# Staggering the two sequences in the pooling passes of a macaron block on eight NeuronCores

## The chip, the cores and the metric

The kernel runs on all 8 cores of one Trainium2 chip. The batch of 16 sequences is split by sequence: each core gets two, runs the same program on them and exchanges nothing with the others. The metric is the device time in microseconds (us) of the slowest core.

## The reference

The input is x of [16, 4096, 1024] float32. Three layers follow one another: half a feed-forward block, attention, half a feed-forward block, each on a layer norm and each added to x.

```python
x = x + 0.5 * ffn(layernorm(x))
x = x + attn(layernorm(x))
x = x + 0.5 * ffn(layernorm(x))

# ffn: D 1024 -> M 64, each of the 64 widened to 16, relu, summed, -> 1024
# attn, per sequence, h = 16 heads of 64:
mixed_q = y @ Wq + bq;  mixed_k = y @ Wk + bk
q_w = softmax((mixed_q @ Wqa + bqa) * scale, axis=1)       # over 4096 tokens
pooled_q = einsum('bsh,bshd->bhd', q_w, mixed_q)           # one row of 1024
mixed_qk = mixed_k * pooled_q
k_w = softmax((mixed_qk @ Wka + bka) * scale, axis=1)
pooled_k = einsum('bsh,bshd->bhd', k_w, mixed_qk)
out = (pooled_k * mixed_q) @ Wt + bt + mixed_q
```

What matters here: the two softmaxes run over all tokens of a sequence, so pooled_q of a sequence is known only after a pass over all of its tokens, the key scores need pooled_q, the key softmax needs the maximum of all key scores, and the output needs pooled_k. The two sequences of a core don't depend on each other.

## The kernel before

Data lie transposed, with the 1024 features as 8 chunks of 128 partitions and the tokens along the free dimension, in tiles of T = 512. A sequence has 8 tiles. "par" is the sequence's number, 0 or 1, and picks its buffers.

The program is written as a list of operations. Each names the keys that it reads and writes; a small planner (Prog) turns them into semaphore waits: a reader waits for the last writer of its key, a writer waits for the last writer and all readers since. Nothing is reordered: each engine and each DMA-issuing queue executes its operations in the order in which the code adds them. So the order of the calls is the order on every engine.

The parts of the program:

1. A dense first part (p1_...): feed-forward, statistics, query scores, and the projections ptq and ptk, which are spilled to DRAM (ptq_d, ptk_d, 1 MB a tile); the query scores go to escq_d.
2. Query pooling (pbq_load, pbq_chain), for each tile: load ptq's tile (1 MB, line 846) and the reciprocal deviation r16 (16 KB, GpSimd's queue, line 482); load the scores esc (32 KB, line 857); ScalarE takes the exponential (line 583); VectorE makes eb (line 595); TensorE spreads eb over the partitions in 8 matmuls (line 601), each followed by a VectorE multiply with a sum (line 606); one add closes the chain (line 615).
3. p1_fin: turns the sums into pooled_q and scales Wka by it (into wkaq_s for sequence 0, wqa_s for 1); p2_init clears the sums.
4. Key scores (p2_load, p2a_chain), for each tile: load ptk's tile (line 931), 8 score matmuls (line 942), and on VectorE the scores, their maximum and the running maximum (lines 552, 556, 559).
5. eb2_final: the bias from the maximum. Key pooling (p2_load, p2b_chain): load ptk's tile again, the 8 score matmuls again, VectorE's esc (line 963), then the same exponential, eb and 8 multiplies as in the query pooling.
6. p2_fin: pooled_k and the output's bias, with 64 small matmuls (line 1010).
7. A dense last part (p3_...): output projection and second feed-forward, one sequence after the other.

In parts 2, 4 and 5 each pass of the loop over ti handles both sequences: it issues the load of tile ti and then runs the chain of tile ti-1, first for sequence 0, then for 1. Sequence 0's loads are issued by SyncE (SP), sequence 1's by ScalarE. The esc load of the query pooling stands in the chain, so on its queue it comes behind the 1 MB load of the next tile. The chain of tile ti-1 comes after the r16 load of tile ti in the order, and waits for it.

Each sequence alternates between two buffers: even tiles in a primary buffer (ptq_s or ptk_s), odd tiles in its half of big_s (tile_buf). The odd buffers of both sequences also share the key "wqT": a load into one half waits for the last load into and the readers of the other half, and a reader waits for both loads.

Of the kernel before, what the change touches and what calls it, by code (L numbers as in the profile page):

```python
# [16 lines left out]
NCH = 8  # L17
# [144 lines left out]
def build_nc(cfg: CFG, dbg=False, paranoid=False, only_p1=False):  # L162
# [60 lines left out]
    with ExitStack() as stk:  # L223
# [33 lines left out]
        ptq_s = sbt("ptq_s", [128, NCH, T], BF16)  # L257
# [311 lines left out]
        def eb2_final(si, side, bias2_ap, bias2_k, tag):  # L569
            base = (si * 2 + side) * 8  # L570
            rmf = base + (cfg.ntile % 2)
            V_op(lambda e: e.tensor_sub(tiny_s[:, base + 7:base + 8], bias2_ap,
                                        tiny_s[:, rmf:rmf + 1]),
                 ["rm%d_%d" % (base, cfg.ntile % 2), bias2_k],
                 ["mx%d" % base], tag + "_eb2")
# [265 lines left out]
        def pbq_load(si, ti):  # L841
            par = si % 2
            t0 = si * cfg.seq + ti * T
            ring = "sync" if par == 0 else "scalar"
            buf, bkeys = pbq_buf(par, ti)
            dma(ring, lambda e: e.dma_start(out=buf[:, :, :],
                                            in_=ptq_r[:, :, t0:t0 + T]),
                ["ptqd_%d" % t0] + bkeys, bkeys, "pbq_pld")
            bcast_r(1, t0, "r16_%d" % par, r16_s[:, par, :], H, "pbq_r16")

        def pbq_chain(si, ti):
            par = si % 2
            t0 = si * cfg.seq + ti * T
            buf, bkeys = pbq_buf(par, ti)
            ring = "sync" if par == 0 else "scalar"
            es = 2 * par + ti % 2
            dma(ring, lambda e: e.dma_start(out=esc_s[:, es, :],
                                            in_=escq_d[:, t0:t0 + T]),
                ["escd_%d" % t0, "escA%d" % es], ["escA%d" % es],
                "pbq_escld")  # L860
            pool_core(si, ti, par, 0, q_slot(si), t0,
                      "pbq_%d_%d" % (si, ti), buf, bkeys)
# [55 lines left out]
                 ["pb_sc", "bka2a"], ["bka2"], "p1_bka2")  # L918

        def p2_buf(par, ti):  # L920
            primary = ((ptk_s, ["ptk_%d" % j for j in range(NCH)])
                       if par == 0
                       else (ptq_s, ["ptq_%d" % j for j in range(NCH)]))
            return tile_buf(primary, par, ti)

        def p2_load(si, ti, tag):
# [259 lines left out]
        if not only_p1:  # L1186
            ti = cfg.ntile - 1
            for si in seqs:
                p1_D1(si, ti)
                p1_D2(si, ti)  # L1190
                for c in range(NCH):
                    p1_D3_j(si, ti, c)
                p1_D3sp(si, ti)
            for si in seqs:
                eb2_final(si, 0, bqa2_s[:], "bqa2", "p1eb2_%d" % si)
            for ti in range(cfg.ntile + 1):
                for si in seqs:
                    if ti < cfg.ntile:
                        pbq_load(si, ti)
                    if ti > 0:  # L1200
                        pbq_chain(si, ti - 1)
            for si in seqs:
                p1_fin(si)
            for si in seqs:
                p2_init(si)
            for ti in range(cfg.ntile + 1):
                for si in seqs:
                    if ti < cfg.ntile:
                        p2_load(si, ti, "p2a_%d_%d" % (si, ti))
                    if ti > 0:  # L1210
                        p2a_chain(si, ti - 1)
            for si in seqs:
                eb2_final(si, 1, bka2_s[:, si:si + 1], "bka2",
                          "p2eb2_%d" % si)
            for ti in range(cfg.ntile + 1):
                for si in seqs:
                    if ti < cfg.ntile:
                        p2_load(si, ti, "p2b_%d_%d" % (si, ti))
                    if ti > 0:
                        p2b_chain(si, ti - 1)  # L1220
            for si in seqs:
                p2_fin(si)
            for sidx, si in enumerate(seqs):
                p3_wtscale(si, reload=(sidx > 0))
                p3_load(si, 0)
                for ti in range(cfg.ntile):
                    if ti + 1 < cfg.ntile:
                        p3_load(si, ti + 1)
                    if ti == 0:
                        p3_wtblock(si, 0)  # L1230
                    else:
                        p3_B(si, ti - 1, filler=mk_p3_filler(si, ti))
                    p3_stats(si, ti)
                p3_B(si, cfg.ntile - 1)
        else:
            def cpout(e):
                return e.dma_start(out=out_d.rearrange("(c p) t -> p c t", p=128)[:, :, 0:T],
                                   in_=x1_bf[:, (cfg.ntile - 1) % 2, :, :])
            dma("gpsimd", cpout,
                ["x1bf%d_%d" % ((cfg.ntile - 1) % 2, j) for j in range(NCH)],  # L1240
                ["outst"], "p1only_out")
# [110 lines left out]
```

How the kernel before makes its waits and increments, by code:

```python
        def run_stream(eng_name, e, clear_sems=None, go=None):  # L118
            if eng_name == "gpsimd":
                for s in clear_sems or ():
                    e.sem_clear(s)
                if go is not None:
                    e.sem_inc(go, 1)
            elif go is not None:
                e.wait_ge(go, 1)
            waited = {}
            def wait_to(skey, val):
                if waited.get(skey, -1) < val:
                    e.wait_ge(sems[skey], val)
                    waited[skey] = val
# [9 lines left out]
                        wait_to((dep.eng, False), dep.val)  # L141
                if op.is_dma:
                    for (ln, occ) in op.lanes:
                        if occ > 1:
                            wait_to((eng_name, "d", ln), 16 * (occ - 1))
                ret = op.emit(e)
                insts = ret if isinstance(ret, (list, tuple)) else [ret]
                if op.is_dma:
                    assert len(insts) == op.ndma, (op.tag, len(insts), op.ndma)
                    for it, (ln, occ) in zip(insts, op.lanes):
                        it.then_inc(sems[(eng_name, "d", ln)], 16)
                elif op.need_inc:
                    insts[-1].then_inc(sems[(eng_name, False)], 1)
            for (eng2, ln), occ in lane_occ.items():
```

## Time and profile before

| | |
|---|---|
| time, 3 runs | 2500.36 us median (2489.80 to 2501.22) |
| profiled execution | 2521.51 us, span of its slowest core 2519.9 us (core 0) |
| spans of the cores | 2475.2 to 2519.9 us |
| TensorE busy (share of span) | 1784.0 us (71%) |
| VectorE busy | 1008.6 us (40%) |
| ScalarE busy | 528.7 us (21%) |
| DMA | 220.28 MB, mean 87 GB/s |
| mean granted TensorE clock, core 0 | 0.803 of full |

How to read it. The profile is one execution; the span is the time from a core's first to its last instruction. Busy shares are means over the whole span and hide that the parts differ. These two lines of the page show the span in 40 equal slices of 63 us, each digit the busy tenths of a slice:

```
PE   0558888888898888888934436666877875877785
DVE  0123333333333333333356524555443443444443
```

Parts 2 to 6 lie in the 20th to the 28th slice. PE is TensorE's matmuls, DVE VectorE, ACT ScalarE, POOL GpSimd, SP SyncE; SPq and ACTq are the DMA queues that SP and ACT issue to. L601 is line 601.

### The profile page before, as it was taken

Reading aid. Unit: us, or ns where it says so; the run is one execution under the profiler, and the core shown is the slowest. Engines: PE = TensorE matmul, PEld = TensorE weight load, DVE = VectorE, ACT = ScalarE, POOL = GpSimd, SP = SyncE. Lnnn points to the kernel's source line nnn. Section 1 sums busy time; section 2 is a strip of 40 time slices with the busy share of each in tenths; the row PEclk is TensorE's granted clock in tenths of the full one; section 3 lists DMA queues with packets and bytes.
Section 4 is the critical chain, followed back from the end, with each engine's and each line's share of the span. In section 5 each row is a group of like instructions: output and inputs, shape, how many; then the busy total and the mean of one; then the engine's idle time right before and its main releaser. Section 6 shows DMA issues by size and latency. Waiting matters only on the chain.

```text
span 2519.9 us, 22407 instructions; the slowest of 8 cores (2475.2 to 2519.9 us)
## 1 busy us (share of the span) xinstructions
PE 1784.0 (71%) x6340; PEld 584.5 (23%) x6340; DVE 1008.6 (40%) x1892; ACT 528.7 (21%) x662; POOL 37.1 (1%) x78
## 2 busy tenths in 40 slices
PE   0558888888898888888934436666877875877785
PEld 0212222222232222222300111112222221222221
DVE  0123333333333333333356524555443443444443
ACT  0232222221222222221000000001322321233232
POOL 0000000000000000000000000000000000000000
PEclk9868998888999999899955565556888876798786
DMA  9212222222112222211243462422224224142411
GB/s 151 61 50 68 84 85 68 84 84 84 45 66 77 85 85 85 68 52 51 64 143 106 140 192 80 115 72 93 71 72 140 73 56 149 52 132 71 130 46 67
DMA packets 174773, 220.28 MB, mean 87 GB/s; under 512 B 6176, under 2 KB 138528, under 8 KB 174016
## 3 DMA queue, kind: packets, MB, share of 16 engines
q1 hardware_dynamic: 126784, 160.15, 20.2%
q10 hardware_dynamic: 44448, 46.70, 5.8%
q0 software_dynamic: 3424, 12.00, 2.9%
q8 instruction: 58, 0.95, 0.2%
q14 instruction: 59, 0.48, 0.1%
HBM read 146.38 MB, written 84.44 MB: 92 GB/s over the span
## 4 chain that ended last, share of the span: by engine, by line
PE 62%; DVE 17%; issue 6%; DMA 6%; ACT 6%; DVEq 1%; ACTq 1%; SPq 0%; POOLq 0%; POOL 0%
PE pb L1063 10%; PE pb L773 9%; PE pb L805 9%; DVE h_bf L606 6%; PE pb L522 4%; PE pb L510 4%; PE pb L942 3%; DVE x_s L1154 3%; PE pb L491 3%; DVE x_bf L691 2%; ACT big_s L717 2%; DMA big_s<-ptk_d 2%; PE pb L725 2%; PE pb L1129 2%; PE pb L535 2%
## 5 line engine op out<-in xcount | busy, mean ns | idle before, releaser
L517 ACT ACTIVATE h_bf<-pb,b1f_s,w1f_s 128x512 bf16<-128x512 f32 x256 | 198.8, 777 | 466.0 <-PE pb L510 466.0
L601 PE MATMUL pb<-eb_s,esel_s 16*128 16x512 bf16 x256 | 141.7, 578 | 170.9 <-DVE eb_s L595 115.5
L773 PE MATMUL pb<-x_bf,wq_s 128*128 128x512 bf16 x1024 | 243.2, 380 | 0.0
L805 PE MATMUL pb<-x_bf,wk_s 128*128 128x512 bf16 x1024 | 243.2, 380 | 0.0
L535 PE MATMUL pb<-g_bf,wout_s 64*128 64x512 bf16 x256 | 129.5, 528 | 97.1 <-DVE x_s L1154 32.8
L816 DVE CAST ptk_s<-pb 128x512 bf16<-128x512 f32 x128 | 88.5, 691 | 270.7 <-PE pb L810 270.7
L522 PE MATMUL pb<-h_bf,w2bd_s 128*64 128x512 bf16 x256 | 110.0, 430 | 84.8 <-ACT h_bf L517 84.8
L1081 DVE TENSOR_TENSOR x_s<-pb,rf_s 128x512 f32<-128x512 f32 x128 | 88.5, 691 | 190.1 <-PE pb L1068 186.6
L1063 PE MATMUL pb<-ptq_s,wt_s 128*128 128x512 bf16 x512 | 132.8, 406 | 17.6 <-DMA ptq_s<-ptq_d 14.0
L784 DVE CAST ptq_s<-pb 128x512 bf16<-128x512 f32 x128 | 87.2, 690 | 137.9 <-PE pb L778 135.7
L1154 DVE SCALAR_TENSOR_TENSOR x_s<-pb,bout_s,x_bf 128x512 f32<-128x512 f32 x128 | 96.0, 750 | 106.2 <-PE pb L535 94.5
L510 PE MATMUL pb<-st_bf,sel_s 64*128 64x512 bf16 x256 | 106.3, 415 | 34.2 <-DVE st_bf L500 34.2
L434 DVE COPY stat_s<-pb 1x512 f32<-1x512 f32 x48 | 32.6, 679 | 241.8 <-PE pb L729 162.5
L1063 PE MATMUL pb<-ptk_s,wt_s 128*128 128x512 bf16 x512 | 129.3, 398 | 0.0
L583 ACT ACTIVATE ee_s<-esc_s,tiny_s 16x512 bf16<-16x512 f32 x32 | 23.0, 720 | 497.5 <-DVE esc_s L963 294.6
L805 PEld LDWEIGHTS pb<-x_bf,wk_s 128*128 128x128 bf16 x1024 | 89.7, 98 | 119.8 <-issue 29.1
L773 PEld LDWEIGHTS pb<-x_bf,wq_s 128*128 128x128 bf16 x1024 | 89.7, 98 | 119.7 <-issue 29.0
L691 DVE SCALAR_TENSOR_TENSOR x_bf<-pb,bout_s,x_s 128x512 bf16<-128x512 f32 x128 | 91.3, 748 | 59.9 <-PE pb L535 56.3
L725 PE MATMUL pb<-x_bf,ones_s 128*1 128x512 bf16 x128 | 54.3, 601 | 84.2 <-ACT big_s L717 84.2
L1092 ACT ACTIVATE big_s<-x_bf 128x512 bf16<-128x512 bf16 x128 | 80.6, 629 | 157.7 <-DVE x_bf L1086 157.5
L448 ACT ACTIVATE stat_s<-stat_s,eps_s 1x512 f32<-1x512 f32 x48 | 34.5, 719 | 344.7 <-DVE stat_s L443 344.6
L1086 DVE SCALAR_TENSOR_TENSOR x_bf<-x_s,btt_s,x_bf 128x512 bf16<-128x512 f32 x128 | 96.2, 751 | 16.3 <-DVE x_s L1081 3.5
(146 smaller groups left out, 1707.5 us busy)
## 6 DMA issues: line engine op xcount, KB each, us to landing
x_s<-xT SPq DMA_DIRECT2D x16, 2048.0 KB, 12.1
out<-x_s SPq DMA_DIRECT2D x16, 2048.0 KB, 8.2
x_d<-x_bf ACTq DMA_DIRECT2D x16, 1024.0 KB
ptq_d<-ptq_s SPq DMA_DIRECT2D x16, 1024.0 KB, 4.4
ptk_d<-ptk_s SPq DMA_DIRECT2D x16, 1024.0 KB, 4.6
x_bf<-x_d SPq DMA_DIRECT2D x16, 1024.0 KB, 14.2
ptq_s<-ptq_d SPq DMA_DIRECT2D x12, 1024.0 KB, 9.4
ptq_s<-ptk_d ACTq DMA_DIRECT2D x8, 1024.0 KB
```

Of the source, the lines that this page charges most:

```text
L510: T_op(lambda e, c=c, eb=eb: e.matmul(pb[eb][:], sel_s[:, c, :], st_bf[:, reg, :], start=True, stop=True), ["st%d" % reg, "sel"], ["pb_e%d ...
L517: S_op(lambda e, c=c, eb=eb: e.activation(out=h_bf[:, c % 2, :], in_=pb[eb][:], func=AF.Relu, bias=b1f_s[:, c:c + 1], scale=w1f_s[:, c:c + ...
L522: T_op(lambda e, c=c: e.matmul(pb[PB_FF][0:FM, :], w2bd_s[:, c, :], h_bf[:, c % 2, :], start=(c == 0), stop=(c == NCH - 1)), ["h%d" % (c % ...
L535: T_op(lambda e, j=j, wb=wb: e.matmul(pb[wb][:], wout_s[:, j * 128:(j + 1) * 128], g_bf[:], start=True, stop=True), ["g", "wout"], ["pb_w% ...
L601: T_op(lambda e, c=c, ebk=ebk: e.matmul(pb[ebk][:], esel_s[:, c, :], eb_s[:, par, :], start=True, stop=True), ["ebbf%d" % par, "esel"], [" ...
L606: V_op(lambda e, c=c, ebk=ebk: e.scalar_tensor_tensor(out=h_bf[:, 0, :], in0=buf[:, c, :], scalar=1.0, in1=pb[ebk][:], op0=ALU.mult, op1=A ...
L691: V_op(lambda e, j=j, wb=wb: e.scalar_tensor_tensor(out=x1_bf[:, par, j, :], in0=pb[wb][:], scalar=bout2_s[:, j:j + 1], in1=x_s[:, par, j, :],
L725: ins.append(e.matmul(pb[PB_S1][0:1, :], ones_s[:, 1:2], x1_bf[:, par, c, :], start=(c == 0), stop=(c == NCH - 1)))
L773: ins = [e.matmul(pb[wb][:], wq_s[:, kc, j * 128:(j + 1) * 128], x1_bf[:, par, kc, :], start=(kc == 0), stop=False) for kc in range(NCH)]
L805: ins = [e.matmul(pb[wb][:], wk_s[:, kc, j * 128:(j + 1) * 128], x1_bf[:, par, kc, :], start=(kc == 0), stop=False) for kc in range(NCH)]
L1063: ins = [e.matmul(pb[wb][:], wt_s[:, kc, j * 128:(j + 1) * 128], qbuf[:, kc, :], start=(kc == 0), stop=False) for kc in range(NCH)]
L1154: V_op(lambda e, j=j, wb=wb: e.scalar_tensor_tensor(out=out_ap[:, j, :], in0=pb[wb][:], scalar=bout2_s[:, j:j + 1], in1=x2_ap[:, j, :], op ...
```

## The change

Only the calls that place parts 2 to 6 are written in another order, and the primary buffers of the key passes are exchanged (sequence 0 now ptq_s, sequence 1 ptk_s), so that each sequence keeps one primary buffer through all passes. No operation is added or removed. Sequence 1 now runs one pass behind sequence 0: query pooling of 0 alone; query pooling of 1 with key scores of 0; key scores of 1 with key pooling of 0; key pooling of 1 alone.

```diff
         def p2_buf(par, ti):
-            primary = ((ptk_s, ["ptk_%d" % j for j in range(NCH)])
+            primary = ((ptq_s, ["ptq_%d" % j for j in range(NCH)])
                        if par == 0
-                       else (ptq_s, ["ptq_%d" % j for j in range(NCH)]))
+                       else (ptk_s, ["ptk_%d" % j for j in range(NCH)]))
             return tile_buf(primary, par, ti)
...
-            for si in seqs:
-                eb2_final(si, 0, bqa2_s[:], "bqa2", "p1eb2_%d" % si)
+            eb2_final(0, 0, bqa2_s[:], "bqa2", "p1eb2_0")
+            eb2_final(1, 0, bqa2_s[:], "bqa2", "p1eb2_1")
             for ti in range(cfg.ntile + 1):
-                for si in seqs:
-                    if ti < cfg.ntile:
-                        pbq_load(si, ti)
-                    if ti > 0:
-                        pbq_chain(si, ti - 1)
-            for si in seqs:
-                p1_fin(si)
-            for si in seqs:
-                p2_init(si)
+                if ti < cfg.ntile:
+                    pbq_load(0, ti)
+                if ti > 0:
+                    pbq_chain(0, ti - 1)
+            p1_fin(0)
+            p2_init(0)
             for ti in range(cfg.ntile + 1):
-                for si in seqs:
-                    if ti < cfg.ntile:
-                        p2_load(si, ti, "p2a_%d_%d" % (si, ti))
-                    if ti > 0:
-                        p2a_chain(si, ti - 1)
-            for si in seqs:
-                eb2_final(si, 1, bka2_s[:, si:si + 1], "bka2",
-                          "p2eb2_%d" % si)
+                if ti < cfg.ntile:
+                    pbq_load(1, ti)
+                    p2_load(0, ti, "p2a_0_%d" % ti)
+                if ti > 0:
+                    pbq_chain(1, ti - 1)
+                    p2a_chain(0, ti - 1)
+            p1_fin(1)
+            p2_init(1)
+            eb2_final(0, 1, bka2_s[:, 0:1], "bka2", "p2eb2_0")
             for ti in range(cfg.ntile + 1):
-                for si in seqs:
-                    if ti < cfg.ntile:
-                        p2_load(si, ti, "p2b_%d_%d" % (si, ti))
-                    if ti > 0:
-                        p2b_chain(si, ti - 1)
-            for si in seqs:
-                p2_fin(si)
+                if ti < cfg.ntile:
+                    p2_load(1, ti, "p2a_1_%d" % ti)
+                    p2_load(0, ti, "p2b_0_%d" % ti)
+                if ti > 0:
+                    p2a_chain(1, ti - 1)
+                    p2b_chain(0, ti - 1)
+            eb2_final(1, 1, bka2_s[:, 1:2], "bka2", "p2eb2_1")
+            p2_fin(0)
+            for ti in range(cfg.ntile + 1):
+                if ti < cfg.ntile:
+                    p2_load(1, ti, "p2b_1_%d" % ti)
+                if ti > 0:
+                    p2b_chain(1, ti - 1)
+            p2_fin(1)
```

ScalarE's queue at the start of the query pooling, before. L846 is the 1 MB load of sequence 1, L857 its esc load, L583 the exponential of either sequence:

```order
L846 DMA ptk_s<-ptq_d 128x8x512
L583 ACTIVATE ee_s,tiny_s<-esc_s,tiny_s 16x512
L846 DMA big_s<-ptq_d 128x8x512
L857 DMA esc_s<-escq_d 16x512
L583 ACTIVATE ee_s,tiny_s<-esc_s,tiny_s 16x512 x2
```

The same place after:

```order
L583 ACTIVATE ee_s,tiny_s<-esc_s,tiny_s 16x512 x8
L846 DMA ptk_s<-ptq_d 128x8x512
L846 DMA big_s<-ptq_d 128x8x512
L857 DMA esc_s<-escq_d 16x512
L583 ACTIVATE ee_s,tiny_s<-esc_s,tiny_s 16x512
L846 DMA ptk_s<-ptq_d 128x8x512
L857 DMA esc_s<-escq_d 16x512
L583 ACTIVATE ee_s,tiny_s<-esc_s,tiny_s 16x512
```

The eight exponentials of sequence 0 now stand in a row ahead of sequence 1's loads; from then on one exponential stands between two of its loads, where there were two, one of each sequence.

VectorE between two query chains, before. L591 and L595 make eb, L606 is the eight multiplies, L615 the closing add:

```order
L591 TENSOR_TENSOR tiny_s<-tiny_s 16x1
L595 TENSOR_TENSOR eb_s<-ee_s,r_s 16x512
L606 SCALAR_TENSOR_TENSOR h_bf,pool_s<-big_s,pb 128x512 x8
L615 TENSOR_TENSOR pool_s<-pool_s 128x8
L591 TENSOR_TENSOR tiny_s<-tiny_s 16x1
```

The same engine after, in the query pooling of sequence 1:

```order
L591 TENSOR_TENSOR tiny_s<-tiny_s 16x1
L595 TENSOR_TENSOR eb_s<-ee_s,r_s 16x512
L606 SCALAR_TENSOR_TENSOR h_bf,pool_s<-ptk_s,pb 128x512 x8
L615 TENSOR_TENSOR pool_s<-pool_s 128x8
L552 TENSOR_TENSOR esc_s<-pb,r_s 16x512
L556 TENSOR_REDUCE tiny_s<-esc_s 16x1
L559 TENSOR_TENSOR tiny_s<-tiny_s 16x1
L591 TENSOR_TENSOR tiny_s<-tiny_s 16x1
```

Where the other sequence's query chain followed, the three instructions of sequence 0's key scores now stand.

TensorE in the key pooling, before. L942 is the eight score matmuls, L601 the eight that spread eb:

```order
L942 MATMUL pb<-ptk_s,wkaq_s 16x512 x8
L601 MATMUL pb<-eb_s,esel_s 128x512 x8
L942 MATMUL pb<-ptq_s,wqa_s 16x512 x8
L601 MATMUL pb<-eb_s,esel_s 128x512 x8
L942 MATMUL pb<-big_s,wkaq_s 16x512 x8
```

The same engine after, in key scores of 1 with key pooling of 0:

```order
L942 MATMUL pb<-ptk_s,wqa_s 16x512 x8
L942 MATMUL pb<-ptq_s,wkaq_s 16x512 x8
L601 MATMUL pb<-eb_s,esel_s 128x512 x8
L942 MATMUL pb<-big_s,wqa_s 16x512 x8
L942 MATMUL pb<-big_s,wkaq_s 16x512 x8
```

Sixteen score matmuls now stand in a row ahead of each chain of sequence 0.

## Rows read from the trace of the kernel before

**Rows 1.** Stages on core 0: stretch, length, busy us, granted clock, DMA share, GB/s.
```profile
core 0: us, PE busy (x) PEld busy (x) DVE busy (x) ACT busy (x) POOL busy (x), PEclk, DMA share, GB/s
1256.50:1425.10 168.60, 71.88 (x128) 12.52 (x128) 99.38 (x308) 12.90 (x32) 7.78 (x16) 0.51 0.42 123
1425.10:1434.10 9.00, 1.00 (x18) 0.74 (x18) 5.99 (x51) 0.00 (x0) 0.00 (x0) 0.50 0.55 159
1434.10:1521.20 87.10, 42.69 (x136) 14.49 (x136) 23.95 (x50) 0.00 (x0) 6.73 (x14) 0.67 0.64 180
1521.20:1718.20 197.00, 121.37 (x249) 26.34 (x248) 110.62 (x324) 13.00 (x32) 6.90 (x15) 0.56 0.35 100
1718.20:1728.40 10.20, 4.01 (x130) 3.78 (x130) 4.01 (x30) 0.00 (x0) 0.00 (x0) 0.50 0.01 2
```

**Rows 2.** Timeline, two query chains in a row: start, us, engine, line, operation.
```profile
1283.36 0.41 DVE L595 TENSOR_TENSOR eb_s<-ee_s,r_s 16x512 bf16<-16x512 bf16 x1
...
1291.39 0.41 DVE L595 TENSOR_TENSOR eb_s<-ee_s,r_s 16x512 bf16<-16x512 bf16 x1
```

**Rows 3.** Timeline around the first stall of the query pooling.
```profile
1307.25 0.17 DVE L615 TENSOR_TENSOR pool_s<-pool_s 128x8 f32<-128x8 f32 x1
...
1307.78 0.47 SPq L857 DMA_DIRECT2D esc_s<-escq_d  x1
1313.29 0.72 ACT L583 ACTIVATE ee_s<-esc_s,tiny_s 16x512 bf16<-16x512 f32 x1 [15.41 <-DMA esc_s<-escq_d]
...
1314.31 0.41 DVE L595 TENSOR_TENSOR eb_s<-ee_s,r_s 16x512 bf16<-16x512 bf16 x1
```

**Rows 4.** DMA issues in the key scores: KB each, median us to landing.
```profile
ptk_s<-ptk_d SPq DMA_DIRECT2D x4, 1024.0 KB, 9.2
```

**Rows 5.** Timeline of the key pooling: first, second and last esc.
```profile
1525.57 0.68 DVE L963 TENSOR_TENSOR esc_s<-pb,r_s 16x512 f32<-16x512 f32 x1 [3.99 <-DMA r_s<-stat_d]
...
1533.98 3.58 PE L942 MATMUL pb<-ptq_s,wqa_s 128*16 128x512 bf16 x8
...
1535.03 0.17 DVE L615 TENSOR_TENSOR pool_s<-pool_s 128x8 f32<-128x8 f32 x1
...
1537.74 0.68 DVE L963 TENSOR_TENSOR esc_s<-pb,r_s 16x512 f32<-16x512 f32 x1 [2.55 <-PE pb L942]
...
1708.44 0.68 DVE L963 TENSOR_TENSOR esc_s<-pb,r_s 16x512 f32<-16x512 f32 x1 [2.12 <-PE pb L942]
```

**Rows 6.** Timeline of the query pooling: its start, and a later add and exponential.
```profile
1262.70 0.38 ACTq L846 DMA_DIRECT2D ptk_s<-ptq_d  x1
1274.36 0.72 ACT L583 ACTIVATE ee_s<-esc_s,tiny_s 16x512 bf16<-16x512 f32 x1 [87.69 <-DMA ptk_s<-ptq_d]
...
1330.20 0.17 DVE L615 TENSOR_TENSOR pool_s<-pool_s 128x8 f32<-128x8 f32 x1
...
1336.70 0.72 ACT L583 ACTIVATE ee_s<-esc_s,tiny_s 16x512 bf16<-16x512 f32 x1 [7.62 <-DMA esc_s<-escq_d]
```

**Rows 7.** Timeline of the first key scores of both sequences.
```profile
1434.16 3.57 PE L942 MATMUL pb<-ptk_s,wkaq_s 128*16 128x512 bf16 x8 [0.47 <-DVE pool_s L976]
...
1437.53 3.13 PE L942 MATMUL pb<-ptq_s,wqa_s 128*16 128x512 bf16 x8
...
1437.98 0.68 DVE L552 TENSOR_TENSOR esc_s<-pb,r_s 16x512 f32<-16x512 f32 x1 [3.83 <-PE pb L942]
...
1439.54 0.15 DVE L559 TENSOR_TENSOR tiny_s<-tiny_s 16x1 f32<-16x1 f32 x1
```

**Rows 8.** Stretches of 2 us in the same row of matmuls, columns as in rows 1.
```profile
1438.00:1440.00 2.00, 2.00 (x6) 0.64 (x5) 1.48 (x3) 0.00 (x0) 0.49 (x1) 0.50 0.04 2
1440.00:1442.00 2.00, 2.00 (x10) 0.81 (x9) 0.99 (x2) 0.00 (x0) 0.00 (x0) 0.99 0.81 138
```

**Rows 9.** Core 3, lines 572 and 974: count, ns min/median/max, first and last start.
```profile
L572 DVE TENSOR_TENSOR tiny_s<-bka_s,tiny_s x2: 140/144/148, 1514.8 to 1515.0; 16x1 f32<-16x1 f32 x2
...
L974 DVE MEMSET tiny_s<- x2: 59/59/59, 1439.4 to 1439.4; 16x1 f32 x2
```

**Rows 10.** DMA issues in the key pooling, columns as in rows 4.
```profile
r_s<-stat_d POOLq DMA_DIRECT2D x15, 16.0 KB, 2.2
```

## The prediction, made before the changed kernel was run

> **What bounds the middle of the kernel now.** I read the busy tenths by slice first: between two dense parts lies a stretch in which no engine and no DMA is busy throughout. A table by stage [rows 1] cuts it into the query pooling (168.6 us), two query finishes (9.0), the key scores (87.1), the key pooling (197.0) and two key finishes (10.2): 471.9 us from 1256.5 to 1728.4, and all that the change touches. Then I read each stage for the wait that ends last.
>
> *Query pooling.* One tile is one DVE chain: eb, eight multiplies, one add. Where nothing is missing the next eb starts 8.03 us after this one [rows 2]; with a short hiccup now and then, 16 chains take (1425.1 - 1275.4 - 3 x 6.9)/16 = 8.06 each. The 6.9 is a stall that comes three times [rows 3]. The row of the last add (1307.25) and that of the next eb (1314.31) lie 7.06 apart instead of 0.2. Between them SP may issue its 1 MB load only once the buffer is free, and issues the small esc load of the tile that is due now behind it, at 1307.78; ScalarE's exponential waits for that until 1313.29. In all other pairs of tiles this latency is there too, but the other sequence's chain (8.06 us) covers it. So the two sequences hide each other's esc load. The stall that is left comes from the key "wqT", which both halves of big_s share.
>
> *Key scores.* PE is busy for half, DVE for a quarter; DMA moves 180 GB/s and a 1 MB load takes 9.2 us to land with the two rings full [rows 1, 4]. The DMA bounds it: 87.1/16 = 5.4 us a tile.
>
> *Key pooling.* Strictly in series: PE scores, DVE esc, ScalarE exp, DVE eb, eight multiplies. The period is (1708.44 - 1525.57)/15 = 12.19 us [rows 5]. PE starts the next score 1.05 us before the add (1533.98 against 1535.03), and esc follows 2.7 us after the add. The loads hide.
>
> **The change, stage by stage.** Nothing is removed; tiles are paired otherwise. I go by core 0. E is the last add of a query chain, F that of a key chain.
>
> *Third 1, query pooling of sequence 0 alone.* The other chain that covered the esc load is gone. Load t+2 is issued at E of chain t, esc t+1 behind it, so each of the gaps after chains 0 to 5 is a bare stall of 6.9; the last esc has no load ahead of it and is hidden. The start: 18.9 us until the first eb, in which four 1 MB transfers (ptk_d's store and three loads) end at 1274.36, 17.9 us after 1256.5; now one of them, ScalarE's of 1262.70, isn't there [rows 6]: 4.4 less. Sum 14.5 + 8 x 8.06 + 6 x 6.9 = 120.4.
>
> *Finish of sequence 0.* 4.5 us, beside the first esc load of sequence 1, which can be issued only behind a big_s load that waits for chain 7: 7.0 to the first eb. That hides the 4.5.
>
> *Third 2, query pooling of 1 with key scores of 0.* The chain's gaps are now on ScalarE's ring: from the add at 1330.20 to the exp at 1336.70 it is 6.5 [rows 6], against SP's 6.04 [rows 3]; from add to eb I take 7.0. Into the gap fall the eight score matmuls (done at E+2.6) and DVE's three instructions (E+2.7 to E+4.4, 1.71 us [rows 7]): free. Before loads of even tiles only the chain's own buffer counts: 8.06 + 7.0, plus 0.9, since key load 0 starts at E+2.6 and shares the engines for the end: 16.0. Before loads of odd tiles "wqT" makes the load wait for the score matmuls too, 2.6 later: 17.6. Three of each: 100.8. Chain 6 to 7 has no stall but DVE's three instructions: 12.2; the last with its scores 12.2. Sum 125.2. The 0.9 lies between 0 (it slips past) and 3 to 4 (a load takes 9.2 where two rings run [rows 4], 5.5 alone); it is nearest to the start times.
>
> *Finish of 1, 4.5.* It has nothing beside it.
>
> *Third 3, key scores of 1 with key pooling of 0.* PE runs 16 score matmuls in a row; the second eight start 3.4 us after the first (1434.16, 1437.53 [rows 7]), so esc of sequence 0 comes 3.4 later: 12.19 + 3.4 = 15.6 a tile; the first 16.7. Loads: for odd tiles both halves of big_s come one after the other, 2 x 6 = 12 us after F, wanted at F+14.5: hidden, by 2.5 us. Sum 16.7 + 7 x 15.6 = 125.9. The granted clock lowers that: it went from 0.50 to 0.99 about 6 us into a row of such matmuls at 1434.16, [rows 7, 8], that is from 1.2 to 2.4 GHz. Sixteen in a row last 6.9 us at the low level, so the last few should run fast: I take 0.9 us a tile, 7 in all. Ends: 0, and 8 x 3.4 = 27 if all run at the high level. Sum 118.9.
>
> The Trainium skill says, in TensorE: Matmul & The Clock Gate, Part 1, that the throttled clock is the default and sustained activity releases it. The trace agrees [rows 8]: 0.50, then 0.99 in the same unbroken row of matmuls.
>
> *Third 4, key pooling of 1 alone.* Finish of key 0 first (5.1), then 13.3 for the first tile and 7 x 12.19 = 85.3, and the last finish 5.1: 108.8. Nothing is gained or lost a tile; the chain was serial already, and its single-ring load has 12 us.
>
> Total 120.4 + 7.0 + 125.2 + 4.5 + 118.9 + 108.8 = 484.8 against 471.9: +13 us on core 0. What the pairing saves is the whole DMA-bound score stage (87.1, now in gaps or as 16 x 3.4 on PE); what it costs is nine more esc stalls (12 against 3, 62 us), the odd tiles' waits, and 27 us of score matmuls in series with the key chain. On core 3 the score stage takes 1439.4 to 1514.8, 75.4 us, 12 less than on core 0 [rows 9]; there the same change costs 25. The slowest core decides; I add 2. The profiled execution took 2521.5 around its span of 2519.9, the median of the runs is 2500.4; the difference is outside these stages or spread over all, so I carry +15 to the median: **2515**.
>
> The weights, buffers and order of the dense parts before and after are the same, so I cost them at nothing. The first loads of the last part could already be issued well ahead (before, 24 us ahead), and are still.
>
> **Rivals.**
> 1. *Forecast, 0.50:* 2515; own range 2504 to 2528.
> 2. *Transfers collide, 0.15:* thirds 2 and 3 each carry two 1 MB loads a tile. If the serial pair of odd loads takes 2 x 9.2 = 18.4 us [rows 4] instead of 12, PE waits 4 for each of three odd tiles, and the esc behind its load comes 3 later in six gaps: 12 + 18 = 30 more, 2545. For: 9.2 was measured with both rings full. Against: here they are full for half of a tile at most.
> 3. *It cancels, 0.27:* the clock is high for most of third 3, as in the second half of the row above (8 x 1 more), and the esc gap in third 2 is 6.3, with no sharing (3 + 4): 15 less, 2500.
> 4. *Faster, 0.08:* the esc load doesn't have to wait behind its 1 MB. A small load on the GpSimd queue landed in 2.2 us in the key pooling [rows 10]; if esc did that where one sequence has the ring to itself, 12 gaps shrink by 5.5 - 2.2 = 3.3: 40 less, 2475. It decides from some 2.5 us a gap. Against: at 1307.78 one sequence had the ring to itself already, and the esc still took 5.5 [rows 3].
>
> The Trainium skill, in DMA: Bandwidth & Descriptors, Queues, rings and completion order, has descriptors consumed in ring order on each engine, but completion not in order of issue. By the first half rival 4 is out; by the second it is open for a load on few engines. The trace has only the 5.5.
>
> **Numbers.** The range 2490 to 2540 leaves out part of rivals 2 and 4. About 0.5% (12.5 us) is what a measurement of this kernel can tell from no change. Slower by more: most of 1 and all of 2, 0.55. Within: a third of 1 and nearly all of 3, less some, 0.37. Faster by more: 0.08.
>
> **What would show it.** ScalarE's exp waiting for DMA esc_s 12 or 13 times, some 6 us each, where before 3 of its waits stopped DVE; third 1 near 120 us; query chains in third 2 alternately 16 and 17.6 apart; key chains in third 3 near 15 with the clock rising inside each row of 16; third 4 at 12.2 a tile; PE never waiting for big_s in third 3. Wrong if esc lands within 3 us of its issue, if third 2 or 3 waits for DMA on score matmuls, or if the parts after 1728 differ in length.

## The result, and the profile after

The changed kernel took 2525.04 us (median of 10 runs), the kernel before 2496.93 (10 runs). The ratio is 1.0103, with a 95% interval from 1.0086 to 1.0119: by this ratio slower by 26 us, and outside the 0.5% that can be told from no change. (The ratio and the spans used below leave out executions in which the cores of one die, or of both, ran at a lower clock.) The profiled execution took 2518.98 us.

```profile
span 2517.0 us, 22296 instructions; the slowest of 8 cores (2495.9 to 2517.0 us)
...
PE pb L1063 9%; PE pb L805 9%; PE pb L773 9%; DVE h_bf L606 5%; PE pb L522 4%; PE pb L510 4%; DMA esc_s<-escq_d 3%; DVE x_s L1154 3%; PE pb L942 3%; PE pb L491 3%; DVE x_bf L691 2%; ACT big_s L717 2%; PE pb L1129 2%; PE pb L725 2%; PE pb L666 2%
```

This is the page's span and, by line, the chain of work that ended last. A load of 32 KB, esc_s, holds 3% of the span on that chain, some 75 us. The stages of core 0 follow, with the columns of [rows 1]: third 1; to the first eb of sequence 1; third 2; finish of 1; third 3; third 4 with its finishes.

```profile
core 0: us, PE busy (x) PEld busy (x) DVE busy (x) ACT busy (x) POOL busy (x), PEclk, DMA share, GB/s
1259.70:1378.40 118.70, 35.93 (x64) 6.25 (x64) 49.90 (x154) 6.50 (x16) 4.82 (x10) 0.51 0.34 101
1378.40:1385.50 7.10, 0.50 (x9) 0.37 (x9) 3.21 (x27) 0.81 (x2) 0.00 (x0) 0.50 0.50 154
1385.50:1513.60 128.10, 63.27 (x128) 13.73 (x128) 61.82 (x177) 5.69 (x14) 6.75 (x14) 0.57 0.44 127
1513.60:1518.20 4.60, 0.92 (x11) 0.54 (x12) 3.10 (x26) 0.00 (x0) 0.51 (x2) 0.64 0.82 234
1518.20:1639.10 120.90, 76.88 (x192) 20.17 (x189) 67.24 (x185) 6.50 (x16) 7.26 (x15) 0.68 0.49 141
1639.10:1748.10 109.00, 66.10 (x258) 17.43 (x258) 59.25 (x190) 6.50 (x16) 2.90 (x6) 0.56 0.31 93
```

They sum to 488.4 us against 471.9. The changed stages of every core, cut at the same instructions:

| us | cores 0 to 7 | median |
|---|---|---|
| before | 471.9 469.9 466.0 462.5 461.7 466.0 465.1 471.9 | 466.0 |
| after | 488.4 481.5 485.0 484.9 492.1 484.9 481.5 481.5 | 484.9 |

That is +18.9, and in these two profiles the median of the eight spans grew by 18.0 (2489.9 to 2507.9). Over more executions it grew by more: the median core took 2486.5 us in 14 executions of the kernel before (timed beside the first experiments) and 2508.4 in 7 of the changed one, 22 apart, and the slowest core 2495.6 and 2520.4, 25 apart. So the changed stages account for 19 of these 25 us. Some 3 lie elsewhere in the middle core and some 3 in how far the slowest core stands from it; no run here locates either.

**The gaps of third 1.** A gap is the time from the closing add of a query chain to the next eb. Timeline of core 0 (columns as in [rows 2]):

```profile
1297.20 0.17 DVE L615 TENSOR_TENSOR pool_s<-pool_s 128x8 f32<-128x8 f32 x1
...
1297.74 0.47 SPq L857 DMA_DIRECT2D esc_s<-escq_d  x1
1302.92 0.72 ACT L583 ACTIVATE ee_s<-esc_s,tiny_s 16x512 bf16<-16x512 f32 x1 [13.75 <-DMA esc_s<-escq_d]
...
1303.94 0.41 DVE L595 TENSOR_TENSOR eb_s<-ee_s,r_s 16x512 bf16<-16x512 bf16 x1
```

It is the stall of [rows 3], 6.7 us, now at six tiles in a row: from eb to eb 14.6 to 14.8 us, and 8.0 for the last pair.

**The gaps of third 2.** A gap with the load of an odd tile (first six rows) and one with the load of an even tile (last two), on core 0:

```profile
1410.35 0.17 DVE L615 TENSOR_TENSOR pool_s<-pool_s 128x8 f32<-128x8 f32 x1
...
1412.91 0.37 ACTq L846 DMA_DIRECT2D big_s<-ptq_d  x1
...
1413.36 0.55 ACTq L857 DMA_DIRECT2D esc_s<-escq_d  x1
...
1421.02 0.36 SPq L931 DMA_DIRECT2D big_s<-ptk_d  x1
1421.21 0.72 ACT L583 ACTIVATE ee_s<-esc_s,tiny_s 16x512 bf16<-16x512 f32 x1 [18.83 <-DMA esc_s<-escq_d]
...
1422.24 0.41 DVE L595 TENSOR_TENSOR eb_s<-ee_s,r_s 16x512 bf16<-16x512 bf16 x1
...
1429.99 0.17 DVE L615 TENSOR_TENSOR pool_s<-pool_s 128x8 f32<-128x8 f32 x1
...
1437.08 0.41 DVE L595 TENSOR_TENSOR eb_s<-ee_s,r_s 16x512 bf16<-16x512 bf16 x1
```

The odd tile's load is issued 2.6 us after the add, when the eight score matmuls are done (the key "wqT"), and the esc behind it then takes 7.9 us instead of 5.2: a gap of 11.9. The even tile's gap is 7.1. The 7.9 can't come from a load on the core's other ring: SP's next one waits for the same key and is issued at 1421.02, when esc is there. It isn't general either. In the three odd gaps esc takes 6.8 to 7.9 us on cores 0 and 4, but 5.4 to 5.9 on the other six, where the odd tile's period (from its eb to the next) is 17.1 to 17.7 us. In the later two even gaps, with a load of the other ring beside it, esc takes 5.6 to 6.1 us on six cores and 6.9 to 8.2 on cores 1 and 5. What makes it slow on some cores is not shown.

**Third 3.** The two rows of eight score matmuls, the add and esc of the key chain, for an even tile (first four rows) and an odd one (last four), and between them two loads that are issued almost together:

```profile
1548.76 3.58 PE L942 MATMUL pb<-ptk_s,wqa_s 128*16 128x512 bf16 x8
...
1549.81 0.17 DVE L615 TENSOR_TENSOR pool_s<-pool_s 128x8 f32<-128x8 f32 x1
...
1552.13 2.06 PE L942 MATMUL pb<-ptq_s,wkaq_s 128*16 128x512 bf16 x8
...
1554.37 0.68 DVE L963 TENSOR_TENSOR esc_s<-pb,r_s 16x512 f32<-16x512 f32 x1
...
1555.35 0.37 ACTq L931 DMA_DIRECT2D ptk_s<-ptk_d  x1
...
1555.64 0.36 SPq L931 DMA_DIRECT2D big_s<-ptk_d  x1
...
1563.73 0.17 DVE L615 TENSOR_TENSOR pool_s<-pool_s 128x8 f32<-128x8 f32 x1
...
1564.10 3.57 PE L942 MATMUL pb<-big_s,wqa_s 128*16 128x512 bf16 x8 [1.35 <-DMA big_s<-ptk_d]
...
1567.47 2.92 PE L942 MATMUL pb<-big_s,wkaq_s 128*16 128x512 bf16 x8
...
1570.56 0.68 DVE L963 TENSOR_TENSOR esc_s<-pb,r_s 16x512 f32<-16x512 f32 x1 [1.00 <-PE pb L942]
```

Stretches of 2 us of the same two tiles (columns as in [rows 1]):

```profile
1552.00:1554.00 2.00, 2.00 (x9) 0.68 (x7) 1.35 (x2) 0.00 (x0) 0.29 (x1) 0.88 1.00 341
...
1567.00:1569.00 2.00, 2.00 (x6) 0.66 (x5) 1.05 (x2) 0.00 (x0) 0.00 (x0) 0.50 0.71 249
```

The even tile's second eight run at 2.4 GHz for most of their time and take 2.06 us; esc follows the add by 4.6. For the odd tile PE first waits 1.35 us for big_s, runs most of its second eight at 1.2 GHz, and esc follows the add by 6.8: 1.4 for the later start, 0.9 for slower matmuls. From eb to eb it is 14.1 or 14.2 us around the even tile and 16.5 around the odd one; two odd tiles have such a wait (1.35 and 1.84 us). PE waits for both halves of big_s, as they share the key. Sequence 1's half, issued at the last add, took 5.9 us (1549.78 to 1555.64); sequence 0's followed it and took 8.5 (1555.64 to 1564.10), beside sequence 1's next load on the other ring.

**Waits** of core 0 over the changed stages, after and then before (total us, times, longest):

```profile
ACT ee_s L583 <- DMA esc_s<-escq_d: 286.2, 14, 83.9
...
DVE tiny_s L591 <- ACT ee_s L583: 103.4, 30, 14.8
...
PE pb L942 <- DMA big_s<-ptk_d: 3.5, 3, 1.8
```
```profile
ACT ee_s L583 <- DMA esc_s<-escq_d: 113.2, 13, 15.4
...
DVE tiny_s L591 <- ACT ee_s L583: 55.7, 20, 18.6
```

The rows of ScalarE say little. The count of ScalarE's waits for esc is nearly the same (14, 13), and in the kernel before most of them cost nothing, as DVE had the other sequence's chain meanwhile. What DVE waits for ScalarE tells it: 103.4 us against 55.7.

### The profile page after: what moved, and what is told of

The parts are those of the page before. It is cut to its first block, busy times and chain, and to the rows that moved or that the text cites. A ratio compares the mean times of both kernels' runs of the same rounds, so it can differ in the third digit from the quotient of the medians.

```text
span 2517.0 us, 22296 instructions; the slowest of 8 cores (2495.9 to 2517.0 us)
## 1 busy us (share of the span) xinstructions
PE 1753.8 (70%) x6246; PEld 580.6 (23%) x6340; DVE 1009.2 (40%) x1892; ACT 528.9 (21%) x662; POOL 37.2 (1%) x78
## 4 chain that ended last, share of the span: by engine, by line
PE 60%; DVE 16%; DMA 9%; issue 7%; ACT 6%; ACTq 1%; DVEq 1%; SPq 0%; POOLq 0%
PE pb L1063 9%; PE pb L805 9%; PE pb L773 9%; DVE h_bf L606 5%; PE pb L522 4%; PE pb L510 4%; DMA esc_s<-escq_d 3%; DVE x_s L1154 3%; PE pb L942 3%; PE pb L491 3%; DVE x_bf L691 2%; ACT big_s L717 2%; PE pb L1129 2%; PE pb L725 2%; PE pb L666 2%
## 5 line engine op out<-in xcount | busy, mean ns | idle before, releaser
L601 PE MATMUL pb<-eb_s,esel_s 16*128 16x512 bf16 x256 | 138.3, 564 | 226.2 <-DVE eb_s L595 168.6
L1063 PE MATMUL pb<-ptq_s,wt_s 128*128 128x512 bf16 x496 | 123.8, 391 | 21.1 <-DMA ptq_s<-ptq_d 15.8
L583 ACT ACTIVATE ee_s<-esc_s,tiny_s 16x512 bf16<-16x512 f32 x32 | 23.0, 720 | 523.1 <-DMA esc_s<-escq_d 287.9
L1063 PE MATMUL pb<-ptk_s,wt_s 128*128 128x512 bf16 x496 | 120.8, 383 | 1.5 <-PE pb L510 1.0
L601 PEld LDWEIGHTS pb<-eb_s,esel_s 16*128 16x128 bf16 x256 | 25.0, 98 | 344.2 <-issue 343.3
## 6 DMA issues: line engine op xcount, KB each, us to landing
x_s<-xT SPq DMA_DIRECT2D x16, 2048.0 KB, 11.9
```

The lines of the kernel that those rows point to most:

```text
L601: T_op(lambda e, c=c, ebk=ebk: e.matmul(pb[ebk][:], esel_s[:, c, :], eb_s[:, par, :], start=True, stop=True), ["ebbf%d" % par, "esel"], [" ...
L1063: ins = [e.matmul(pb[wb][:], wt_s[:, kc, j * 128:(j + 1) * 128], qbuf[:, kc, :], start=(kc == 0), stop=False) for kc in range(NCH)]
```

## The experiments

Theory: the esc load stands behind a 1 MB load on its in-order queue, and the other sequence's chain no longer covers that. Rivals: the shared key "wqT", transfers that collide, and the score matmuls in series. "Stages" is the median over the cores of the changed stages (466.0 before, 484.9 after). Ratios are to the kernel before, timed beside each run.

**a_esc and b_esc: the esc load ahead of its own 1 MB load.** After (a) and before (b):

```
 def pbq_load(si, ti):
     buf, bkeys = pbq_buf(par, ti)
+    es = 2 * par + ti % 2
+    dma(ring, ... out=esc_s[:, es, :], in_=escq_d[:, t0:t0 + T] ...)   # out of pbq_chain
     dma(ring, ... out=buf[:, :, :], in_=ptq_r[:, :, t0:t0 + T] ...)
```

> The changed kernel with one edit: the esc load of a tile is issued in the load step, ahead of that tile's own 1 MB load, one pass earlier than before. Theory Q (the gaps of 6.9 us are the esc load, which waits on its queue for the buffer and then behind the next 1 MB): all gaps go. First third 119 to about 77 us (start 12, then 8 x 8.06), second 128 to about 99 (8 x 12.3, the chain plus DVE's three score instructions), start of the second 7.1 to 4.5: 70 to 75 us less than the changed kernel's 2525, so about 2452, ratio to before 0.982. Rival C (contention of two 1 MB loads a tile makes the second and third thirds long): only the first third shrinks, 42 less, 2483. Rival L (the wait after a chain is a fixed cost of issue and exponential): 2525, no change.

> The same edit in the kernel before. Theory Q: there the other sequence covers all gaps but three, so only these three stalls (3 x 6.9 = 21 us) and perhaps 3 us of the start go: 2473 to 2478, ratio 0.991. Then the staggered order with the esc load early would be some 20 to 25 us faster than the order of before with it: the sign of the change hangs on where one small load stands. Rival C: the stalls there come from the shared key of big_s and its two serial loads, not from esc: no change, 2497, and the staggered order stays behind.

Measured: a_esc 2448.85 us, ratio 0.9801 (0.9780 to 0.9823), stages 412.1; b_esc 2470.64, 0.9883 (0.9858 to 0.9908), stages 438.6. The gap in third 1 of a_esc (core 2) is 0.21 us:

```profile
1274.16 0.17 DVE L615 TENSOR_TENSOR pool_s<-pool_s 128x8 f32<-128x8 f32 x1
...
1274.37 0.41 DVE L595 TENSOR_TENSOR eb_s<-ee_s,r_s 16x512 bf16<-16x512 bf16 x1
1274.69 0.47 SPq L847 DMA_DIRECT2D esc_s<-escq_d  x1
```

The load issued at 1274.69 is that of the tile after next. Third 1 falls from some 120 to 73 us, third 2 from 132 to 102 (core 2). One edit takes 73 us out of the staggered stages and 27 out of the old ones, and turns the pairing from a loss of 19 into a gain of 26. That shows the theory for the gaps. Third 3, which has no esc load, keeps its length (117.8 us on core 2, 117.4 in the changed kernel), and with it whatever the loads cost there.

**a_swap: how much of the gap is lying behind the 1 MB, how much being issued late.** In the changed kernel, esc of tile t+1 gets the waits of load t+2, but is issued just ahead of it (shortened):

```
 def pbq_chain(si, ti): ...
+    q = p.ops.pop()                    # the esc load
+    i = <the last pbq_pld on this ring>
+    q.deps += p.ops[i].deps
+    p.ops.insert(i, q)
```

> The changed kernel with the esc load made to wait for exactly what the next tile's 1 MB load waits for, but issued just ahead of it instead of just behind. It separates the two halves of the gap: waiting to be issued (kept) and lying behind 1 MB on the queue (taken away). Theory Q with the ring in order: esc lands in 2 to 2.5 us instead of 5.5, each of 12 gaps is about 3.2 shorter, 38 us less than 2525: 2487, ratio 0.996. If a small load takes 5.5 whatever is ahead of it: 2525, ratio 1.011. If it slips past the 1 MB anyway: the same 2525.

Measured: 2479.31 us, ratio 0.9895 (0.9863 to 0.9928), stages 430.4. That is 54 us less in the stages, where 38 had been expected: 24.5 in third 1's gaps, as much from there to the last query chain, 4 in the start (medians of the cores). Third 1 of core 2:

```profile
1291.62 0.17 DVE L615 TENSOR_TENSOR pool_s<-pool_s 128x8 f32<-128x8 f32 x1
1291.65 0.32 SPq L857 DMA_DIRECT2D esc_s<-escq_d  x1
...
1293.54 0.72 ACT L583 ACTIVATE ee_s<-esc_s,tiny_s 16x512 bf16<-16x512 f32 x1 [9.95 <-DMA esc_s<-escq_d]
...
1294.56 0.41 DVE L595 TENSOR_TENSOR eb_s<-ee_s,r_s 16x512 bf16<-16x512 bf16 x1
```

The gap is 2.9 us here, 6.7 in the changed kernel and 0.2 in a_esc. So 3.8 us come from standing behind the 1 MB load and 2.7 from being issued only when its buffer comes free. Issued first, esc is there 1.9 us after its issue, near the 2.2 of r_s in [rows 10]; behind the big load it takes 5.2. The Trainium skill says (DMA: Bandwidth & Descriptors, Queues, rings and completion order) that each DMA engine takes descriptors in ring order. The changed kernel and a_swap agree with that, with 5.2 against 1.9 us.

**a_nokey and b_nokey: the two halves of big_s without the key "wqT".**

```
-            keys = (["sq0", "u", "wqT"] if par == 0
-                    else ["sq1", "sqP3", "wqT"])
+            keys = (["sq0", "u"] if par == 0
+                    else ["sq1", "sqP3"])
```

> The changed kernel with the key wqT, which ties the two halves of big_s together, left out of the odd tiles' buffers. Theory: query loads of odd tiles need no longer wait for the other sequence's score matmuls, so the three long periods of the second third (18 to 19.6) fall to the short ones (15): 9 to 12 us less; in the last two thirds PE's 1.2 to 1.5 us waits for big_s go, 4 less: about 2511, ratio 1.005. Rival C: the key also keeps two 1 MB loads apart; without it they run together, the esc load behind one of them lands 3 us later and nothing is gained: 2525.

> The kernel before without the key wqT in the odd tiles' buffers. Theory K (the three stalls of 6.9 us in its query pooling come only since the key delays a big_s load by one chain; otherwise the other sequence's chain of 8.06 us covers the whole esc gap of 6.9): they go, 21 us less, 2476, ratio 0.991. Rival: the esc load behind its 1 MB is the cause by itself: the stalls stay, 2497. The key scores are bound by DMA and keep their length by both.

Measured: a_nokey 2497.44 us, ratio 1.0004 (0.9988 to 1.0019), stages 464.6; b_nokey 2463.41, 0.9866 (0.9844 to 0.9888), stages 428.1. Both gained more than expected. Thirds 2 and 3 on core 2, changed kernel and then a_nokey:

```profile
1382.70:1515.20 132.50, 63.79 (x139) 14.15 (x140) 64.96 (x202) 6.51 (x16) 7.32 (x16) 0.55 0.46 134
1515.40:1632.80 117.40, 71.09 (x191) 19.36 (x189) 67.24 (x185) 6.50 (x16) 7.06 (x15) 0.73 0.51 143
```
```profile
1374.40:1496.50 122.10, 63.78 (x139) 14.14 (x140) 64.95 (x202) 5.70 (x14) 7.25 (x15) 0.57 0.47 143
1496.70:1607.40 110.70, 71.30 (x191) 19.39 (x189) 67.16 (x185) 6.51 (x16) 7.26 (x15) 0.75 0.55 155
```

The work is the same, the time 10 and 7 us less. In third 3 every tile after the first two now takes 13.7 us, and PE has no wait for big_s left. On the kernel before, the key had cost the three stalls (pooling 169 to 146) and, which I had not expected, a part of the key scores. Core 2, before and then b_nokey:

```profile
1444.70:1525.20 80.50, 41.61 (x136) 14.15 (x136) 24.09 (x55) 0.00 (x0) 6.77 (x14) 0.71 0.68 194
```
```profile
1420.00:1485.50 65.50, 37.72 (x133) 12.79 (x134) 24.05 (x56) 0.00 (x0) 6.75 (x14) 0.84 0.85 241
```

The DMA share rises from 0.68 to 0.85. I had read that stage as bound by the DMA; a fifth of its time went with the key, in which one ring had waited for the other's load and its reader. The Trainium skill puts SP's and ScalarE's rings on the same 16 engines (DMA: Bandwidth & Descriptors, Issuing engines are not separate DMA queues). These rows don't speak against that: the same loads moved at 241 GB/s instead of 194 once they could overlap, so the gain is filled idle time.

**a_esc_nokey, its repeat a_esc_nokey2, and b_esc_nokey: both edits together.**

> The changed kernel with both the early esc load and without the key wqT. With the esc load early the second third waits for nothing of the key any more (12.1 a tile), so of the key's 20 us only the last thirds' should be left to gain: third 3 from 118 to 111, 7 to 10 us less than with the early esc load alone (2449): 2441, ratio 0.977. Rival (the two effects add): 20 less, 2429, 0.972. Rival C (loads collide without the key): no gain, 2449.

> The staggered order with both edits again, beside the order of before with both on the same chip, since its first interval was wide: 2436 to 2444, ratio 0.977, 15 to 20 us under the other.

> The kernel before with both edits, the early esc load and no key wqT, so that the two orders are compared with both of the causes gone. Without the key alone the query pooling took 147 us and the key scores 63 (428 for all stages, 466 before). With esc early as well only the start of the pooling can shrink, from some 18 to 8 or 10 us: 420, time about 2457. The staggered order with the same two edits took 399.8: it is then about 20 us faster, as it puts the DMA-bound 63 us of key scores beside other work and pays 1.4 x 8 = 11 on TensorE, 1.7 to 4 a tile on VectorE in the second third, for it. Rival (the stagger's gain is only the early esc load): both at the same time.

Measured: a_esc_nokey 2447.66 us, ratio 0.9787 (0.9726 to 0.9848), stages 399.8; b_esc_nokey 2452.74, 0.9828 (0.9813 to 0.9843), stages 418.2. The repeat's four times lay between 2435.97 and 2546.72 us, too far apart for a ratio, so as a time it is inconclusive; its stages were 399.8 again. The interval of a_esc_nokey also covers a_esc's ratio (0.9801), so that the second edit gains on top of the first is shown by the stages alone (412.1 to 399.8). The stages together:

| stages, us | before | staggered | pairing |
|---|---|---|---|
| as they were | 466.0 | 484.9 | +18.9 |
| without the key | 428.1 | 464.6 | +36.5 |
| esc first | 438.6 | 412.1 | -26.5 |
| both | 418.2 | 399.8 | -18.4 |

The sign of the change hangs on where esc is issued. The key makes all four kernels slower but doesn't set the sign: without it the old pairing gains even more (38 us against 20), and with esc first the staggered one is ahead with the key and without.

**a_fill3, a_all and a_fill3b: the score matmuls put into PE's waits.** In third 3 (a_fill3), or in 2 and 3 (a_all, with both edits above), one score matmul of the other sequence follows each of the eight that spread eb, as a filler of PE's wait for the multiply. a_fill3b is a_fill3 with sequence 0's loads issued first in third 3.

```
                      tag + "_em%d" % c)
+                if filler is not None:
+                    filler(c)      # one score matmul of the other sequence
                 V_op(lambda e, c=c, ebk=ebk: e.scalar_tensor_tensor(
```

> The changed kernel; in the third third only, the eight score matmuls of sequence 1 are put one by one between the eight spreading matmuls of sequence 0's key chain, where TensorE waits for VectorE's multiplies, instead of ahead of the chain. Theory S (the score matmuls in series cost 1.4 us a tile at the clock they get, and the odd tiles another 2.5 to 3 for big_s): the even periods fall from 13.9 to 12.3, the odd from 16.5 to about 13: 16 to 20 us less than 2525, 2507, ratio 1.004. Rival: the matmuls lengthen the spreading ones (0.43 + 0.43 in a slot of 0.80 at the low clock) and the multiplies wait, 0.1 to 0.3 a slot: only 5 to 10 less.

> The changed kernel with the early esc load, without the key wqT, and with the key score matmuls put between the spreading matmuls in the second and the last but one third. The second third becomes VectorE's chain of 8.06 and three score instructions of 1.7 with nothing between them: 9.8 to 10.5 a tile (2 MB in it is 200 GB/s, about what DMA gave in the key scores before), about 86 instead of 100; the third one 12.4 a tile, 101 instead of 111: 24 less than the last one, about 2418, ratio 0.968. Rival C (DMA bounds the second third at 5.4 us a MB): 11 a tile, 8 us later, 2426. Rival T (the high clock of the unbroken score rows is lost and the chain's matmuls are slower): the third one stays at 111, 2430.

> The changed kernel with the scores put between the spreading matmuls in the third third, as in the run that was 42 us slower than before, and one edit more: in each pass of that third the loads of sequence 0 are issued before those of sequence 1, on all queues. Theory P (of the 25 us which that run lost in the third third, most came from GpSimd's queue: its r16 load of sequence 1 waits for VectorE's scores, which now come after the chain, and holds back the r16 load of sequence 0 behind it, so that esc waits 3.9 to 5.5 us a tile): the wait goes, third 3 falls from 143 to 110 to 118, about 2510. Theory M (the matmul slots of 1.06 instead of 0.80 us are the loss: 8 x 8 x 0.26 = 17): it stays near 135. By both together: 143 - 8 x 4 = 111 at best, as the slots' 17 stay and the 1.4 a tile of serial scores go.

Measured: a_fill3 2538.82 us, ratio 1.0170 (1.0148 to 1.0192); a_all 2464.74, 0.9870 (0.9847 to 0.9893); a_fill3b 2524.48, 1.0102 (1.0085 to 1.0119). The expectations of all three failed: third 3 takes 143 us on core 2 of a_fill3, where 117 stood, and 146 in a_all. Two waits stand in a_fill3's timeline:

```profile
1540.63 0.69 DVE L608 SCALAR_TENSOR_TENSOR h_bf<-big_s,pb 128x512 bf16<-128x512 bf16 x1 [0.36 <-PE pb L601]
...
1541.45 0.59 PE L967 MATMUL pb<-big_s,wqa_s 128*16 128x512 bf16 x1
1541.69 0.69 DVE L608 SCALAR_TENSOR_TENSOR h_bf<-big_s,pb 128x512 bf16<-128x512 bf16 x1 [0.36 <-PE pb L601]
...
1548.17 0.96 POOL L482 DMA_DIRECT2D r_s<-stat_d  x2 [18.16 <-DVE esc_s L552]
...
1552.63 0.68 DVE L986 TENSOR_TENSOR esc_s<-pb,r_s 16x512 f32<-16x512 f32 x1 [3.94 <-DMA r_s<-stat_d]
```

First, at the low clock a spreading matmul and a score matmul together outlast the multiply: it is 1.06 us from multiply to multiply (0.80 in the changed kernel), and DVE waits 0.36 for PE in each. From eb to the add it is 9.6 us (1554.45 to 1564.08) instead of 7.5 (1556.19 to 1563.73 in the changed kernel's third 3). The granted clock of the stage falls from 0.73 to 0.56. Second, sequence 1's esc now comes at the chain's end, and with it the time at which its r_s may be reloaded; sequence 0's small r_s load stands behind it on the GpSimd queue, and DVE waits 3.9 us. a_fill3b puts that load ahead; there the same instruction waits for PE only, but ScalarE has a new wait:

```profile
1556.76 0.37 ACTq L933 DMA_DIRECT2D big_s<-ptk_d  x1
1557.28 0.72 ACT L583 ACTIVATE ee_s<-esc_s,tiny_s 16x512 bf16<-16x512 f32 x1 [15.73 <-DMA big_s<-ptk_d]
...
1570.66 0.68 DVE L986 TENSOR_TENSOR esc_s<-pb,r_s 16x512 f32<-16x512 f32 x1 [0.87 <-PE pb L944]
```

Its third 3 is 125 us, 18 less, so most of the 26 lost came from the queue. What the longer row from eb to the add costs isn't separated, as the new order has a cost of its own. The exponential of three odd tiles now stands on ScalarE behind sequence 1's load into big_s, which by the key waits for sequence 0's, and there DVE waits 3.2 to 5.8 us for it instead of 1.1 on the eight cores (3.8 to 4.6 on core 2): some 9 us.

**a_best: both edits, and the filler in third 2 alone**, where DVE has nothing else to do in the chain's gap.

> The staggered order with both edits, and the key score matmuls of sequence 0 between the spreading matmuls in the second third only, where they brought it from 101.3 to 97.6 us. 4 us less than with the two edits alone: 2433 to 2440, ratio 0.975; a difference at the edge of what can be told.

Measured: 2426.75 us, ratio 0.9725 (0.9706 to 0.9745), stages 396.4. It is faster than both kernels, 69 us below the one before (2495.46 beside it). Third 2 on core 2:

```profile
1337.80:1435.50 97.70, 69.01 (x139) 12.40 (x140) 64.74 (x205) 5.69 (x14) 7.26 (x15) 0.50 0.56 174
```

Most tiles of third 2 take 11.6 us; in a_esc_nokey they take 12.0 to 12.5, the stage 101.9. So the filler is worth 4.2 us in this third and 3.4 in all the stages (399.8 to 396.4). The expectation had 2433 to 2440; the rest of this ratio's lead over a_esc_nokey's lies outside the stages, within that run's wide interval.

## Why the prediction was right, step by step

It forecast slower for the reason found: 2515 us, +15, where +26 was measured; the time of 2525.04 lies inside its range of 2490 to 2540, 10 us above the forecast, and inside the forecast's own range of 2504 to 2528. Its steps, on core 0:

| us | predicted | measured |
|---|---|---|
| third 1 | 120.4 | 118.7 |
| to the first eb of 1 | 7.0 | 7.1 |
| third 2 | 125.2 | 128.1 |
| finish of 1 | 4.5 | 4.6 |
| third 3 | 118.9 | 120.9 |
| third 4 | 108.8 | 109.0 |
| sum | 484.8 | 488.4 |

- *Third 1, right.* The six long periods are 14.6 to 14.8 us, stalls of 6.5 to 6.8 against 6.9. They are gone in a_esc, which changes only when and where esc is issued, so they are esc's.
- *Third 2, 2.9 short on core 0.* Even tiles took 14.8 or 14.9 us (16.0 predicted; the first 17.1), odd ones 18.4 to 19.7 (17.6). The 16.0 was too long there: esc takes 5.7 or 5.8 us in the even gaps, and the 0.9 for sharing isn't seen in the gap. The 17.6 is what six cores have (17.1 to 17.7); on cores 0 and 4 the slower odd esc adds 1 to 2, for a reason that is not shown. The two errors partly cancel in the sum, which is luck.
- *Third 3, the sum nearly right, two terms wrong against each other.* I took the serial scores as 3.4 us a tile, less 0.9 for the clock; with no load late (a_nokey) a tile takes 13.7, only 1.5 over 12.19, so the clock gave about 1.9. It rose earlier than I had read: 0.88 of full over 1552 to 1554, in a row begun at 1548.76. But "hidden, by 2.5 us" failed: I had taken 2 x 6 us for the two halves of big_s, and they took 5.9 and 8.5. PE waited 1.35 and 1.84 us before two odd tiles on this core (3.1 and 3.7 on core 2), and lost part of the clock's gain with it. A wait of third 3 for DMA was one of the signs that the prediction had named for being wrong, and it came true in this small part.
- *The step that was mis-sized most: from core 0 to the time.* I had worked out that the change costs core 3 some 25 us where it costs core 0 13, and then added 2. Measured were 22.4 and 16.5. Core 0 was the slowest in the profile shown, and with 471.9 us in these stages among the two slowest. Against the median core's 466.0 my own sum gives 484.8 - 466.0 = 18.8, where 18.9 was measured; that it agrees so well is luck, as the sum was made for core 0, which took 488.4. The cores differ as much after (481.5 to 492.1) as before (461.7 to 471.9), but not in the same order.
- *The last part.* I cost it at nothing. From the end of the changed stages to the span's end it was 762.1 us before and 766.5 after (medians over cores). The prediction had named a different length there as a sign of being wrong. But in the experiments, which leave that part alone, it was 762.4 to 769.0, and the 769.0 is b_esc's, with the old pairing. So these 4 us are not shown to be the change's.
- *Rival 2, collision*, wanted esc 3 us later in six gaps and PE waiting 4 for odd tiles. The second half happened at a part of its size: the waits of PE are 3.1 to 6.9 us in all on the eight cores, behind loads on both rings. Of the first half, esc was up to 2.7 later in the odd gaps of cores 0 and 4, but with no other 1 MB load of the core in flight. The sum of 2545 did not come.
- *Rival 3, it cancels*, had the clock right (8 x 1 more) and the gaps of even tiles nearly; it fell on the odd tiles.
- *Rival 4, esc slips past*, is refuted by 5.2 us behind the big load. Its price was right, though: issued ahead, esc takes 1.9, which is 3.3 less a gap, and a_swap gained 54 us in the stages where this rival had counted 40 for 12 gaps.
- *What the prediction called for as proof*, 12 or 13 waits of ScalarE for esc, was a poor sign, as the kernel before has 13 such waits too; it was the wait of DVE for ScalarE that told.

For the key the prediction had counted 17.6 - 16.0 in three gaps, 5 us. It costs 20 in the changed stages (484.9 to 464.6): on core 2 it is 10 in third 2, where the loads of odd tiles were issued late, and 7 in third 3, where PE waited; the other 3 lie in the start of third 1, which differs by as much from core to core.

## What to carry to other kernels

Before two interleaved streams are paired otherwise, list each small load that stands behind a large one on an in-order queue, and ask which stream's work covers its latency now; here the coverage was worth 45 us (73 less 27), more than the 26 that the new pairing gains without it. Issue the small load that is needed first ahead of the large one that waits for a buffer, and look for keys that tie independent buffers together. A stage whose DMA share is 0.68 isn't shown to be bound by the DMA while its loads wait for each other; and what a filler costs in a chain is counted at the clock that the mixed row of matmuls gets. Work that is summed for one core is set against the median core, not against the slowest of one profile.

## What the runs showed of the hardware that I had not expected

- A wait of 1.35 us on PE went with an esc 2.3 us later: 1.4 late, and 0.9 because the second eight matmuls then took 2.92 us instead of 2.06.
- Sixteen score matmuls in a row ran part of their second half at 0.88 of the full clock or more (1552 to 1554 us of core 0), the stage at 0.73 on core 2. Put one by one between others they left the same stage at 0.56 (a_fill3), with 0.59 us each.
- A 32 KB load took 1.9 us ahead of a 1 MB load on its ring and 5.2 behind it. In sequence 1's query pooling it took 5.6 to 6.1 us on six cores with a 1 MB load issued some 2.2 us later on the other ring (6.9 to 8.2 on two), and 5.4 to 5.9 on six cores without one (6.8 to 7.9 on the other two). What makes the slow ones isn't shown.
- Two rings whose loads no longer waited for each other moved 241 GB/s in the key scores, where they had moved 194 (core 2).
